# A scan kernel in one core: skip products in another step, normalisation work exchanged between two engines, fewer convolution strips on VectorE

## The reference, cut to what matters

```python
# layer 0: group norm, layer norm, gated attention along rows
x = x + _L0_conv_ref(_gn(x), ...)
# layer 1: group norm, then
xi, z = jnp.split(x @ w_in.T, 2, axis=-1)            # 256 + 256 channels
xc = silu(depthwise_conv3x3(xi) + conv_b)
for k in range(4):        # rows, columns, and both backwards
    dts, Bs, Cs = split(x_proj_w[k] @ xs[k])
    delta = softplus(dt_w[k] @ dts + dt_b[k])
    h = exp(delta * A) * h + delta * x * B           # 16 states for each of 256 channels
    y = sum over states of (h * C) + Ds * x
y = layernorm(sum of the four directions) * silu(z)
x = x + y @ w_out.T
```

## Time and profile before

| | us |
|---|---|
| median of 3 runs | 25642.71 (25639.85 to 25644.08) |
| the profiled execution | 25641.48 |
| its span | 25639.6 |
| VectorE busy | 24801.7 (97%) |
| ScalarE busy | 23485.8 (92%) |
| TensorE busy (matmuls) | 22994.3 (90%) |
| GpSimd busy | 20394.3 (80%) |
| mean granted clock of TensorE | 0.987 of full speed |

### The profile page before, as it was taken

How to read it: one execution, slowest core, us unless ns; L and a number is a source line. 1 busy time by engine, 2 the same in 40 slices (tenths; PEclk the granted TensorE clock), 3 DMA queues, 4 the chain that set the end, 5 groups by cost and what they waited for, 6 DMA issues and landing times. The chain is left out here.

```text
span 25639.6 us, 503079 instructions
## 1 busy us (share of the span) xinstructions
PE 22994.3 (90%) x187532; PEld 19842.2 (77%) x187532; DVE 24801.7 (97%) x25540; ACT 23485.8 (92%) x48015; POOL 20394.3 (80%) x7116
## 2 busy tenths in 40 slices
PE   3997889999999999999999999999999999999989
PEld 1775458888888888888888888888888888888877
DVE  8998989999999999999999999999999999999996
ACT  2997579999999999999999999999999999999986
POOL 3000049999999999999999899999998999999987
PEclk7998999999999999999999999999999999999999
DMA  4222554444444455555555555555555555555555
GB/s 155 72 61 93 175 174 169 166 168 167 168 167 169 164 181 178 180 179 180 180 179 181 173 175 177 176 178 176 175 177 173 176 179 176 175 177 175 179 176 190
DMA packets 2918225, 4287.36 MB, mean 167 GB/s; under 512 B 1199422, under 2 KB 2250722, under 8 KB 2635874
## 3 DMA queue, kind: packets, MB, share of 16 engines
q1 hardware_dynamic: 2915810, 4255.17, 49.7%
HBM read 3660.03 MB, written 594.54 MB: 166 GB/s over the span
## 5 line engine op out<-in xcount | busy, mean ns | idle before, releaser
L1299 DVE TENSOR_TENSOR_SCAN s_h<-s_da,s_h,s_db 128x512 f32<-128x512 f32 x16256 | 19392.8, 1259 | 217.1 <-PE s_db L1198 182.5
L1320 POOL TENSOR_TENSOR s_prod<-s_h,s_cb 128x2048 f32<-128x2048 f32 x4096 | 18657.8, 4569 | 1079.4 <-issue 661.9
L1259 ACT ACTIVATE s_da<-s_delta,a_neg 128x512 f32<-128x512 f32 x16384 | 10871.0, 712 | 430.9 <-DVE s_h L1299 430.8
L1248 ACT ACTIVATE s_dxb<-s_dx,s_btok 128x256 f32<-128x256 f32 x22528 | 9794.4, 497 | 67.1 <-PEq L59 67.1
L1195 PE MATMUL s_db<-eye,s_dxb 128*128 128x128 f32 x49152 | 8215.2, 276 | 1370.9 <-DVE s_h L1299 1260.1
L1211 PE MATMUL s_py<-eye,s_prod 128*128 128x128 f32 x65536 | 8604.9, 273 | 456.2 <-DVE s_yt L1286 329.3
L1195 PEld LDWEIGHTS s_db<-eye,s_dxb 128*128 128x128 f32 x49152 | 5696.6, 142 | 2891.0 <-issue 1853.0
L1211 PEld LDWEIGHTS s_py<-eye,s_prod 128*128 128x128 f32 x65536 | 7427.4, 141 | 579.1 <-DVE s_yt L1286 419.1
L1198 PE MATMUL s_db<-s_bdiag,s_dx 128*128 128x128 f32 x32768 | 6338.7, 275 | 0.0
L1198 PEld LDWEIGHTS s_db<-s_bdiag,s_dx 128*128 128x128 f32 x32768 | 4951.7, 191 | 0.0
L1333 POOL TENSOR_SCALAR s_dxb<-s_dx,s_btok 128x256 f32<-128x256 f32 x2048 | 997.5, 487 | 797.0 <-PE s_db L1198 796.3
(11 more groups left out here) (134 smaller groups left out, 15647.0 us busy)
## 6 DMA issues: line engine op xcount, KB each, us to landing
s_cb<-c_rows SPq DMA_DIRECT2D x2048, 1024.0 KB, 4.8
s_bdiag<-b_diag SPq DMA_DIRECT2D x2048, 256.0 KB, 4.4
s_xt<-xc_tok SPq DMA_DIRECT2D x1024, 256.0 KB, 5.2
y<-s_yt SPq DMA_DIRECT2D x1024, 256.0 KB, 2.1
s_xc<-xc_own SPq DMA_DIRECT2D x384, 512.0 KB, 7.3
s_yb<-y SPq DMA_DIRECT2D x768, 256.0 KB, 3.8
xc_tok<-c_ot SPq DMA_DIRECT2D x32, 2048.0 KB, 8.8
xc_own<-s_xc SPq DMA_DIRECT2D x128, 512.0 KB, 5.8
```

The source lines that it names most:

```text
L1248: last = e.activation(dxb[:, i % NDXB, j, :], dx[:, g % 2, j, :], ACT.Copy, scale=btok[:, g % 2, j, n:n + 1])
L1259: last = e.activation(da[:, i % NDA, half, :], delta[:, g % 2, half, :], ACT.Exp, scale=wts[k]["a_neg"][:, half, n:n + 1])
L1299: last = e.tensor_tensor_scan(h[:, n, half, flow], da[:, i % NDA, half, flow], db[:, i % NDB, half, flow], first, ALU.mult, ALU.add)
L1320: e.tensor_tensor(prod[:, p % GROUPS_KEPT], h[:, states], cb[:, states, :].unsqueeze(2).to_broadcast([P, TOGETHER, HALVES, T]), ALU.mult). ...
```

## The change

There are three edits.

1. In the normalisation GpSimd and VectorE exchange work. VectorE now scales and shifts the tile (two instructions of 128 x 2048), GpSimd normalises the 16 blocks with 16 instructions of 128 x 128 and signals after every fourth, and TensorE waits for each four blocks instead of the tile. VectorE waits, before it overwrites `rstd` of a tile, for GpSimd to be done with the tile two before.
2. `SHARED` goes from 4 to 8: VectorE computes half 0 only of every eighth strip (72 instead of 80 strips in all), TensorE the others (56 instead of 48).
3. The skip products follow the total of state 4 (`GROUP`) instead of state 0, and `load_own` is issued one group of states later.

```diff
             @block.gpsimd
             def _(e):
                 for q in range(N):
-                    s, g = q % LOADS, q % AFFINE
-                    e.wait_ge(S[f"load{s}"], 2 * DMA * (q // LOADS + 1))
+                    s, g = q % 2, q % AFFINE
+                    e.wait_ge(S["nmr"], q + 1)
+                    for j in range(BLOCKS):
+                        last = e.tensor_scalar(gt[:, g, j, :], gt[:, g, j, :], rstd[:, s, j:j + 1], nmr[:, s, j:j + 1],
+                                               ALU.mult, ALU.add)
+                        if j % 4 == 3:
+                            last.then_inc(S["normed"], 1)
+
+            @block.vector
+            def _(e):
+                def begin(q):
+                    s, g, l = q % 2, q % AFFINE, q % LOADS
+                    e.wait_ge(S[f"load{l}"], 2 * DMA * (q // LOADS + 1))
                     if q >= AFFINE:
                         e.wait_ge(S["turned"], 4 * (q - AFFINE) + 4)
-                    e.tensor_tensor(four(gt[:, g]), four(xt[:, s]), row(scale_row), ALU.mult).then_inc(S["scaled"], 1)
+                    e.tensor_tensor(four(gt[:, g]), four(xt[:, l]), row(scale_row), ALU.mult).then_inc(S["scaled"], 1)
                     e.wait_ge(S["scaled"], q + 1)
                     e.tensor_tensor(four(gt[:, g]), four(gt[:, g]), row(shift_row), ALU.add).then_inc(S["shifted"], 1)
...
                 def finish(q):
-                    s, g = q % 2, q % AFFINE
+                    s = q % 2
                     e.wait_ge(S["std"], q + 1)
+                    if q >= 2:
+                        e.wait_ge(S["normed"], 4 * (q - 2) + 4)
                     e.reciprocal(rstd[:, s], std[:, s]).then_inc(S["rstd"], 1)
...
-                    e.wait_ge(S["nmr"], q + 1)
-                    for j in range(BLOCKS):
-                        last = e.tensor_scalar(gt[:, g, j, :], gt[:, g, j, :], rstd[:, s, j:j + 1], nmr[:, s, j:j + 1],
-                                               ALU.mult, ALU.add)
-                    last.then_inc(S["normed"], 1)
...
-                    e.wait_ge(S["normed"], q + 1)
                     for f in range(4):
+                        e.wait_ge(S["normed"], 4 * q + f + 1)
...
-    SHARED = 4
+    SHARED = 8
...
-                            if q == 0 and prepares(g + 2) and kept(g + 2):
+                            if q == 1 and prepares(g + 2) and kept(g + 2):
                                 load_own(g + 2)
...
-                        if n == 0 and k in SKIP:
+                        if n == GROUP and k in SKIP:
```

More of the change, by code:

```diff
@@ L191, in _ @@
                 for q in range(N):
-                    s, g = q % LOADS, q % AFFINE
-                    e.wait_ge(S[f"load{s}"], 2 * DMA * (q // LOADS + 1))
-                    if q >= AFFINE:
-                        e.wait_ge(S["turned"], 4 * (q - AFFINE) + 4)
-                    e.tensor_tensor(four(gt[:, g]), four(xt[:, s]), row(scale_row), ALU.mult).then_inc(S["scaled"], 1)
-                    e.wait_ge(S["scaled"], q + 1)
-                    e.tensor_tensor(four(gt[:, g]), four(gt[:, g]), row(shift_row), ALU.add).then_inc(S["shifted"], 1)
+                    s, g = q % 2, q % AFFINE
[5 more added lines that the diff above has]
+                            last.then_inc(S["normed"], 1)
             @block.vector
@@ L202, in begin @@
                 def begin(q):
-                    s, g = q % 2, q % AFFINE
+                    s, g, l = q % 2, q % AFFINE, q % LOADS
+                    e.wait_ge(S[f"load{l}"], 2 * DMA * (q // LOADS + 1))
+                    if q >= AFFINE:
+                        e.wait_ge(S["turned"], 4 * (q - AFFINE) + 4)
+                    e.tensor_tensor(four(gt[:, g]), four(xt[:, l]), row(scale_row), ALU.mult).then_inc(S["scaled"], 1)
+                    e.wait_ge(S["scaled"], q + 1)
+                    e.tensor_tensor(four(gt[:, g]), four(gt[:, g]), row(shift_row), ALU.add).then_inc(S["shifted"], 1)
                     e.wait_ge(S["shifted"], q + 1)
```

## The result

| | before | after |
|---|---|---|
| median of the runs (before with one more) | 25641.57 us (4 runs, 25639.85 to 25644.08) | 25297.49 us (4 runs, 25295.14 to 25303.17) |
| profiled execution | 25641.5 us | 25295.7 us |
| its span | 25639.6 us | 25293.9 us |

What follows compares the result with a forecast made beforehand. VectorE was taken to bound the kernel, busy 883 of 945 us in the convolution and setting the scans' pitch, with GpSimd excluding it in the normalisation. 25641.5 - 149 - 12 - 223 = 25257.5, forecast 25258 us, range 25195 to 25370.

Steps and rivals of the forecast that it cites:

- the pitch of the two engines: Normalisation: GpSimd's 5.8 us plus 5.1 us kept out by VectorE make a tile pitch of 10.9 us.
- part 1: Normalisation, GpSimd and VectorE exchanging work: 149 us gained, with ends of 52 and 168.
- the forecast's own sign of being wrong: Normalisation: a tile pitch over 12 us would show the forecast wrong.
- That adds at most 0.3 us: Normalisation: the wait for a tile's buffers to go round, 21 to 24 us against two pitches of 21.8.
- time kept out by VectorE: Normalisation: VectorE instructions exclude GpSimd for 4.6 us of scale and shift, some 0.4 small ones, 0.1 hand-overs: 5.1 us.
- The short instruction: Normalisation rival: GpSimd's 128-element instruction costs 0.56 us like the long one, pitch 14.1, gain 52, time 25355; chance 0.07.
- the two engines don't starve each other: Normalisation rival denied here: starving engines add GpSimd's 5.8 to VectorE's 9.6 us, pitch 15.4, time 25402; chance 0.05.
- Part 2: Convolution, eight strips moved from VectorE to TensorE: 12 us gained, between 15 lost and 40 gained.
- leaves that as it is: Convolution: the same code and lead of four pairs keep TensorE's stands at 7.3 us, now per group of eight.
- Part 3: Scans of directions 2 and 3, skip products moved four steps later: 0.88 us per tile, 223 us gained.
- Both margins: Scans, skip's new place: TensorE's work ready 1.0 us before the scan and 1.4 us before VectorE wants delta's transposes.
- The late load: Scans rival: the moved column load misses its reader, 384 us per microsecond, time from 25642 up; chance 0.02.

Runs made afterwards that it cites:

- half the blocks: The changed kernel with GpSimd normalising only every second block, 8 instructions per tile instead of 16, the others left unnormalised: 25207.61 us, ratio 0.9830.
- both mends: The changed kernel with five input buffers instead of three and ScalarE's square root issued earlier, before its copies, in the normalisation: 25244.5 us.
- The lead of six: The changed kernel with LAG = 6 instead of 4 in the convolution, so TensorE transposes results back six pairs behind: 25259.19 us, ratio 0.9850.

## Why the prediction was right, and where it was not

Three things came about as forecast: the pitch of the two engines in the normalisation, TensorE as the bound of the convolution, and the covered skip products. The sum lies within the range. But 54 us of part 1 are missing, and the forecast's own sign of being wrong, a normalisation pitch over 12 us, was met.

**Part 1, the normalisation: 149 us forecast, 95.3 measured. The step that failed is the one on the buffers, "That adds at most 0.3 us".** The other steps:

| step | forecast | measured |
|---|---|---|
| pitch before | 15.54 us | 15.54 from normalising to normalising, 15.65 from figures to figures |
| pitch after, with the round trips | 10.9 us | 12.71 from normalising to normalising, 12.57 from figures to figures |
| wide VectorE instruction | 2.3 us | 2.3 to 2.4 |
| VectorE's work of a tile | 9.6 us | 9.85 with waits (half the blocks) |
| 16 narrow GpSimd instructions | 5.8 us | 6.9 |
| time kept out by VectorE | 5.1 us | 4.0 |
| pitch of the two engines | 10.9 us | 10.87 (both mends) |
| round trips on top | at most 0.3 us | 1.7 (12.57 - 10.87) |
| first normalising instruction earlier by | 7 us | 9.0 (173.6 to 164.6) |
| last tile, from its first normalising instruction, longer by | 1.6 us | 1.3 |

Counted as the forecast counts, the gain is 31 x 2.826 + 9.0 - 1.3 = 95.3 us. 31 tiles of 1.7 us are the 53 us that the two mends gave back. That the pitch of the two engines came out at 10.9 was luck: the narrow instructions took 1.1 us more than forecast and the time kept out 1.1 us less. Either error alone would have moved the gain by 31 x 1.1 = 34 us. I had taken the old order of the queues as it stood, where the load was issued 10 us after the normalisation's end, and had let the sum "21 to 24 us" meet "two pitches, 21.8 us" with no slack. But a quantity of up to 24 us against 21.8 is no margin, and the landing's spread comes on top: a late load delays the figures, these delay GpSimd, and that delays the next load. The load is the last thing in a chain (GpSimd, TensorE, ScalarE, the store of the bias) whose first member the change had just made longer. And I didn't look at ScalarE's square root at all, which has the same chain in front of it. At the end of the stage the same lateness shows once more: from the last figures to the end it takes 21.7 us, 5.8 more than before, since at 554.0, when the last figures are there, GpSimd has 27 of the 32 instructions of the last two tiles still to do (the row of 551.90 above).

Of the two rivals for this part neither came about. The short instruction is 0.45 us and not 0.56, and the two engines don't starve each other: the pitch would have been 15.4. The exclusion itself is seen in the longest instruction of 2.58 us. The Trainium skill has this rule (SBUF — State Buffer, "Who interferes with whom"), and the trace agrees that the two exclude each other; the excluded time is some 2.0 to 2.1 us, though, and not the whole 2.3 to 2.4 us of the recorded instruction. The Trainium skill's warning that moving work between these two engines might not help (Perfetto Trace Analysis, "Optimizing Scalar/DVE Operations") is not borne out here: an exchange, in which the narrow instructions went to GpSimd and the wide ones to VectorE, took 95 us off a stage of some 530.

**Part 2, the convolution: 12 us forecast, 22.4 measured for the strips, 24.0 with the ends.** The mechanism was right: TensorE became the bound and kept its stands, and VectorE waits for the copies, though in half of its strips (36 waits, 72 strips) and not in most. The forecast had eight groups of 114.2 us, 914 in all; the strips took 904.7. From start to start the first seven groups take 113.8 us on average, 0.4 less than forecast, and the last one takes 107.9, 6.3 less: that the groups are not alike was the larger error. Within groups two to seven two terms were mis-sized and nearly made up for each other: the stands are 6.2 us and not 7.3, because the second one shrank from 4.84 to 3.16 us in four of the six, and what is left for the clock is 113.8 - 104.9 - 6.2 = 2.7 us, not 2. So "leaves that as it is" holds for the place of the stands and not for their length. The lead of six showed what they hang on: TensorE's waits at line 757 fell from 55.3 to 21.5 us, 10.1 of it the first stand of the stage.

**Part 3, the scans: 223 us forecast, 226 measured.** The pitches of directions 2 and 3 are 41.25 and 41.24 us, direction 0's is 41.26. Both margins held. The first one, 1.0 us in the working, is 1.1 us in the trace, and the skip products take 0.90 us and not 0.99, so a second round of them leaves 0.2 us.

**The late load:** not seen. In the page's group of TensorE's projection (line 964) 18.1 us of waiting for `xc_own` are listed, and they are the one wait at the very start of the scans, which the kernel before has too (18.8 us):

```profile
L964 PE MATMUL s_pr<-s_xc,w_proj 128*73 128x512 f32 x2048 | 963.9, 593 | 18.8 <-DMA s_xc<-xc_own 18.1
```

**The sum.** -384 was forecast and -345.7 measured: 54 us too much in part 1, 12 too little in part 2, 3 too little in part 3. So the errors of parts 2 and 3 hid 15 us of the one in part 1.

## What to carry to other kernels

When a stage gets faster, its buffers have to come round faster too: follow one buffer from its last use through every queue to its reload, add it up with the new durations, and call it covered only if the sum of the slow cases is below the pitches it has. When two waits of a stage open the same gap, the gain of taking each away is not additive, so test both together before ruling on either. An exchange of narrow and wide work between GpSimd and VectorE can pay even though they exclude each other, and for a small step that must be done somewhere on a queue, the place counts more than the time: the same 0.9 us a tile cost 228 us in all three states earlier and nothing where they stand, even twice.

## What the runs showed of the hardware that was not expected

**The exclusion is shorter than the instruction.** A recorded VectorE product of 2.3 to 2.4 us kept GpSimd out for 2.0 to 2.1 us, and beside the statistics and small instructions GpSimd kept its 0.43 us from start to start.

**TensorE's clock can fall after a short stand, too, and not every time.** The forecast tied a lower clock to the stand of 4.8 us. In the kernel after it is so in the groups that have a stand of 4.84 us: behind the one of 2.46 us the window gives full clock, behind the one of 4.84 us 0.65 (length, busy of PE, granted clock, DMA share, GB/s):

```profile
2837.70:2842.50 4.80, 4.80 (x17) 0.65 0.12 36
2818.60:2824.00 5.40, 5.31 (x31) 1.00 0.84 275
```

In the five groups whose second stand is 3.16 us the clock falls behind the 2.46 us already. Two of them:

```profile
2591.20:2594.20 3.00, 3.00 (x14) 0.61 0.74 276
2703.50:2706.50 3.00, 3.00 (x14) 0.67 0.73 274
```

In two of these five it is low again behind the 3.16 us (the row at 2722.49 above has 0.69 us for two transposes instead of 0.44). With a lead of six only the short stand is left, and the clock falls behind it too. The window (busy of PE, PEld, DVE, ACT and POOL ahead of the clock):

```profile
2906.90:2910.00 3.10, 3.08 (x13) 2.62 (x14) 3.03 (x3) 1.73 (x3) 0.00 (x0) 0.57 1.04 342
```

and three of its rows in the timeline, the clock falling some 0.4 us behind the stand and back by the last one:

```profile
2906.92 0.44 PE L757 MATMUL c_op<-eye,c_xc 128*128 128x128 f32 x2 [2.47 <-ACT c_xc L803]
2907.49 0.63 PE L757 MATMUL c_op<-eye,c_xc 128*128 128x128 f32 x2
2911.68 0.38 PE L757 MATMUL c_op<-eye,c_xc 128*128 128x128 f32 x2
```

0.57 is a mean over the window, near the lower level of 1.2 GHz. The stretch from 2906.92 to 2911.68 takes 4.76 us, and the same work at full clock 3.09 us (2818.69 to 2821.78 in the kernel after): 1.7 us a group. With it the group of 109.1 us is explained, 104.9 + 2.5 + 1.7. Why the clock falls behind a stand of 2.46 us in one group and not in the next, under the same code, stays open; no run was made for it.
